# An eight-expert layer: every token through every expert in split precision, against tokens sorted by expert and moved by indirect transfers

## The reference

```python
logits_BSE = jnp.einsum('BSD,DE->BSE', x, router_kernel_DE)
probs_BSE = jax.nn.softmax(logits_BSE.astype(jnp.float32), axis=-1)
weights_BSK, indices_BSK = jax.lax.top_k(probs_BSE, TOP_K)          # TOP_K = 2 of E = 8
norm_weights_BSK = jax.nn.softmax(weights_BSK, axis=-1)
one_hot_BSKE = jax.nn.one_hot(indices_BSK, num_classes=E, dtype=x.dtype)
full_weights_BSE = jnp.sum(one_hot_BSKE * norm_weights_BSK[..., None], axis=2)
gating_BSEF = jnp.einsum('BSD,EDF->BSEF', x, kernel_gating_EDF)     # D = 256, F = 512
act_BSEF = jax.nn.silu(gating_BSEF)
up_BSEF = jnp.einsum('BSD,EDF->BSEF', x, kernel_up_EDF)
fuse_BSEF = act_BSEF * up_BSEF
down_BSED = jnp.einsum('BSEF,EFD->BSED', fuse_BSEF, kernel_down_EFD)
out_BSD = jnp.einsum('BSED,BSE->BSD', down_BSED, full_weights_BSE)
```

## Time and profile before

| | |
|---|---|
| median of 3 runs | 1378.36 us (1377.51 to 1386.43) |
| profiled execution, device time | 1375.61 us |
| its span in the trace | 1373.7 us |
| its mean granted TensorE clock | 0.891 of full speed |
| first work of the expert stage | 655.35 us |
| end of its last normalisation | 1033.46 us |

### The profile page before, as it was taken

One profiled execution on the slowest core, in us unless ns is written; L12 is line 12 of the kernel. 1 busy time (PEld: TensorE's weight loads), 2 busy tenths in 40 slices (PEclk: granted clock), 3 DMA queues, 4 the chain that ended last, 5 costly groups with the idle time before them and its releaser, 6 DMA issues. The chain is left out here.

```text
span 1373.7 us, 29227 instructions
## 1 busy us (share of the span) xinstructions
PE 1106.4 (81%) x11509; PEld 922.8 (67%) x11509; DVE 728.2 (53%) x1538; ACT 547.3 (40%) x1059; POOL 391.0 (28%) x466
## 2 busy tenths in 40 slices
PE   5899364899976565898889999999995899998373
PEld 5787233777753354786689999999994677777231
DVE  4467375566646997465254433434364445443374
ACT  2344271656527762453434232333221333332550
POOL 0222154444314442223211211211105444432102
PEclk9999586999988787999799999999998799996675
DMA  5100201000001000200110111030001000000001
GB/s 177 66 3 3 97 1 65 1 1 0 1 3 34 1 0 1 94 3 2 47 47 1 47 46 46 5 126 0 0 1 68 2 3 3 3 3 1 1 1 36
DMA packets 11140, 35.64 MB, mean 26 GB/s; under 512 B 3026, under 2 KB 5795, under 8 KB 9362
## 3 DMA queue, kind: packets, MB, share of 16 engines
q1 hardware_dynamic: 11026, 34.06, 7.0%
HBM read 32.84 MB, written 1.21 MB: 25 GB/s over the span
## 5 line engine op out<-in xcount | busy, mean ns | idle before, releaser
L147 PE MATMUL psum<-L2f_XT_high,L2f_EW_high 128*128 128x444 f32 (+1 forms) x384 | 136.8, 356 | 9.0 <-issue 5.1
L1929 ACT ACTIVATE L2f_act<-psum 128x444 f32<-128x444 f32 (+1 forms) x96 | 48.9, 511 | 222.6 <-PE psum L147 222.5
L147 PE MATMUL psum<-L2f_XT_high,L2f_EW_low 128*128 128x444 f32 (+1 forms) x384 | 134.8, 351 | 0.0
L147 PE MATMUL psum<-L2f_XT_low,L2f_EW_high 128*128 128x444 f32 (+1 forms) x384 | 134.3, 350 | 0.0
L2008 DVE TENSOR_TENSOR L2f_prod<-psum,L2f_act 128x444 f32<-128x444 f32 (+1 forms) x96 | 55.8, 582 | 148.1 <-ACT L2f_act L1929 148.1
L1894 POOL TENSOR_TENSOR L2f_EW_low<-weights_even,L2f_EW_high 128x1024 fp32r<-128x1024 f32 x24 | 58.1, 2424 | 265.5 <-ACT L2f_EW_high L1908 265.5
L147 PE MATMUL psum<-L2f_EW_high,L2f_H_high 128*111 128x256 f32 x352 | 99.3, 282 | 2.6 <-issue 2.6
L147 PE MATMUL psum<-L2f_EW_low,L2f_H_high 128*111 128x256 f32 x352 | 98.8, 281 | 0.0
L147 PE MATMUL psum<-L2f_EW_high,L2f_H_low 128*111 128x256 f32 x352 | 98.4, 280 | 0.0
L147 PEld LDWEIGHTS psum<-L2f_XT_high,L2f_EW_high 128*128 128x128 f32 x384 | 73.4, 191 | 15.5 <-issue 8.5
L147 PEld LDWEIGHTS psum<-L2f_XT_high,L2f_EW_low 128*128 128x128 f32 x384 | 73.3, 191 | 3.9
(11 more groups left out here) (359 smaller groups left out, 2797.0 us busy)
## 6 DMA issues: line engine op xcount, KB each, us to landing
weights_even<-experts SPq DMA_DIRECT2D x8, 1536.0 KB, 6.5
weights_even<-L_w SPq DMA_DIRECT2D x4, 1024.0 KB
patch_ring<-patches SPq DMA_DIRECT2D x11, 333.0 KB, 3.6
weights_odd<-L_wqkv SPq DMA_DIRECT2D x2, 768.0 KB
out<-X SPq DMA_DIRECT2D x10, 111.0 KB
weights_odd<-L_wo SPq DMA_DIRECT2D x1, 1024.0 KB, 9.9
weights_even<-tok_w SPq DMA_DIRECT2D x1, 768.0 KB
weights_even<-L_wg SPq DMA_DIRECT2D x1, 768.0 KB, 4.3
```

Of the source, the lines that this page charges most:

```text
L147: mm = core.nc.tensor.matmul(out, left[a], right[b], start=first and n == 0, stop=last and n == len(passes) - 1)
L1929: nc.scalar.activation(act_[:, p, 0:k * R], core.bank(p)[:, 0:k * R], ACT.Silu).then_inc(act_done, 1)
```

## The change

Each token's two (token, expert) pairs become two slots in a list sorted by expert, where each expert begins on a multiple of 128. The list has at most (2 x 1221 + 8 x 127) / 128 = 27 tiles of 128 slots (`NS`), and the program always runs 27. One expert serves a whole tile.

- SyncE copies `X` to DRAM twice, as `expert_rows` and as `expert_sums`, and loads all eight experts (12.6 MB) at the start of the stage. It then loads the next stage's weights, waits for the last addition, and reads `expert_sums` back into `X`.
- The ranks come from matmuls with matrices of ones, and the list from 22 matmuls that turn marks into the token (`source`, `target`) and weight (`wslot`) of each slot. VectorE makes the marks; it does some 35 instructions more than `route` did, and nothing runs beside them but the transfers.
- GpSimd gathers 128 rows for each tile into a ring of three buffers (`xs`) and adds 128 rows for each tile into `expert_sums`, by indirect transfers. An addition waits for the landing of the one before it.
- TensorE works in plain fp32 with one call for a product where it had three: per tile two transposes, two gate calls and two up calls of 512 columns, four transposes of the hidden tile, four down calls of 256 columns. The expert's number is read from SBUF into a register of TensorE (`value_load`) and picks the columns of `EW`.

Core of the diff, with the list's arithmetic left out:

```diff
+NS = (2 * TOK + 8 * 127) // 128
...
             @block.sync
             def _(sp):
-                with sp.Fori(0, (NEX - 2) // 2) as j:
-                    for u in range(2):
-                        sp.wait_ge(w_low, j * 6 + 3 * (u + 1))
-                        sp.dma_start(raw[u], core.dram["experts"][j * 2 + (2 + u)]).then_inc(we[u], 16)
+                for p in SPLIT:
+                    sp.dma_start(by_tile(rows, p, 0, NT), X[p, :, :]).then_inc(rows_out, 16)
+                for e in range(NEX):
+                    sp.dma_start(EW[:, e, :], core.dram["experts"][e]).then_inc(w_in, 16)
+                for p in SPLIT:
+                    sp.dma_start(by_tile(sums, p, 0, NT), X[p, :, :]).then_inc(sums_out, 16)
                 load_next(sp, next_loads, next_sem)
+                sp.wait_ge(added, 16 * NS)
+                for g, (t0, k) in enumerate(GROUPS):
+                    for p in SPLIT:
+                        sp.dma_start(X[p, t0:t0 + k, :], by_tile(sums, p, t0, k)).then_inc(back[g], 16)
...
             @block.gpsimd
             def _(pool):
...
+                def gather(j):
+                    if j == 0:
+                        pool.wait_ge(rows_out, 32)
+                        pool.wait_ge(source_done, 1)
+                    after(pool, x2_ps, j - 2)
+                    nc.gpsimd.indirect_dma_start(xs[:, j % 3, :], None, rows[:, :],
+                                                 bass.IndirectOffsetOnAxis(ap=source[:, j:j + 1], axis=0)).then_inc(got[j % 3], 16)
+
+                def scatter(j):
+                    if j == 0:
+                        pool.wait_ge(sums_out, 32)
+                        pool.wait_ge(target_done, 1)
+                    pool.wait_ge(y_done, j + 1)
+                    after(pool, added, 16 * j)
+                    nc.gpsimd.indirect_dma_start(sums[:, :], bass.IndirectOffsetOnAxis(ap=target[:, j:j + 1], axis=0), Y[:, j % 2, :], None,
+                                                 compute_op=ALU.add).then_inc(added, 16)
+
+                for j in range(3):
+                    gather(j)
+                for j in range(NS):
+                    scatter(j)
+                    if j + 3 < NS:
+                        gather(j + 3)
                 tail.pool(pool)
...
             @block.vector
             def _(dve):
...
+                def weigh(j):
+                    dve.wait_ge(y_ps, j + 1)
+                    after(dve, added, 16 * (j - 1))
+                    V.tensor_scalar(Y[:, j % 2, :], core.bank(5)[:, 0:D], wslot[:, j:j + 1], None, ALU.mult).then_inc(y_done, 1)
...
+                for g in range(len(GROUPS)):
+                    dve.wait_ge(back[g], 32)
+                    tail.stats(g)
+                for g in range(len(GROUPS)):
+                    tail.norm(dve, g)
...
             @block.tensor
             def _(pe):
...
+                def x_T(j):
+                    pe.wait_ge(got[j % 3], 16 * (j // 3 + 1))
+                    after(pe, x2_done, j - 1)
...
+                for j in range(NS + 1):
+                    if j + 1 < NS:
+                        x_T(j + 1)
+                    if j < NS:
+                        expert[j] = pe.value_load(expert_of[0:1, j:j + 1], min_val=0, max_val=NEX - 1)
+                        if j == 0:
+                            pe.wait_ge(w_in, 16 * NEX)
+                        pe.wait_ge(x2_done, j + 1)
+                        after(pe, silu_done, j - 1)
+                        half(j, j % 2, 0, g_ps)
+                    if j >= 1:
+                        pe.wait_ge(prod_done, j)
+                        after(pe, ht_done, j - 1)
+                        for c in range(4):
+                            mm = nc.tensor.transpose(core.bank(4)[:, c * 128:(c + 1) * 128], H[:, (j - 1) % 2, c * 128:(c + 1) * 128], core.ident[:, :])
+                        mm.then_inc(ht_ps, 1)
+                    if j < NS:
+                        after(pe, prod_done, j - 1)
+                        half(j, 2 + j % 2, KD * NF, u_ps)
+                    if j >= 1:
+                        pe.wait_ge(ht_done, j)
+                        after(pe, y_done, j - 1)
+                        for c in range(4):
+                            mm = nc.tensor.matmul(core.bank(5)[:, 0:D], HT[:, (j - 1) % 2, c * 128:(c + 1) * 128],
+                                                  EW[:, expert[j - 1], 2 * KD * NF + c * D:2 * KD * NF + (c + 1) * D], start=c == 0, stop=c == 3)
+                        mm.then_inc(y_ps, 1)
```

More of the change, by code:

```diff
@@ L1857, in experts_ffn @@
-        we = [we0, we1]
+        hot, spot = sb("hot", [128, 2, NT, NEX]), sb("spot", [128, 2, NT, NEX])
+        both, rank = sb("both", [128, NT, NEX]), sb("rank", [128, NT, NEX])
+        need = sb("need", [128, 8, NEX])
+        slot, which, inside = sb("slot", [128, 2, NT]), sb("which", [128, 2, NT]), sb("inside", [128, 2, NT])
+        ended, owner = sb("ended", [128, NS, NEX]), sb("owner", [128, NS])
+        expert_of = sb("expert_of", [128, NS], I32)
+        mark, empty, wslot = sb("mark", [128, NS]), sb("empty", [128, NS]), sb("wslot", [128, NS])
@@ L2100, in body @@
[L2100 to L2110 removed]
+                pe_transpose_x(core, pe, xt_ps, lambda t, c: X[:R, t, c * 128:(c + 1) * 128], core.ident[:R, :R], False, xt_done)
@@ new lines, in _ @@
+                for t in range(NT):
+                    pe.wait_ge(xt_done, t // 2 + 1)
+                    for c in range(KD):
+                        mm = nc.tensor.matmul(core.bank(0)[:R, t * NEX:(t + 1) * NEX], XT[:, c, t * R:(t + 1) * R], router[:, c, :],
+                                              start=c == 0, stop=c == KD - 1)
+                mm.then_inc(lg_ps, 1)
+                pe.wait_ge(both_done, 1)
+                pe.wait_ge(set_up, 1)
+                flat = both[:R].rearrange("p t e -> p (t e)")
@@ new lines, in _, with x_T, half @@
+                mm.then_inc(mark_ps, 1)
+                pe.wait_ge(owner_done, 1)
+                def x_T(j):
+                    pe.wait_ge(got[j % 3], 16 * (j // 3 + 1))
+                    after(pe, x2_done, j - 1)
+                    for c in range(KD):
+                        mm = nc.tensor.transpose(core.bank(6 + j % 2)[:, c * 128:(c + 1) * 128], xs[:, j % 3, c * 128:(c + 1) * 128], core.ident[:, :])
+                    mm.then_inc(x2_ps, 1)
+                def half(j, bank, first, sem):
+                    for c in range(KD):
+                        mm = nc.tensor.matmul(core.bank(bank), xsT[:, j % 2, c, :], EW[:, expert[j], first + c * NF:first + (c + 1) * NF],
+                                              start=c == 0, stop=c == KD - 1)
+                    mm.then_inc(sem, 1)
```

392 lines of the change are left out of this document (169 added, 223 removed).

## The result

| | before | after |
|---|---|---|
| median | 1377.93 us (4 runs, 1373.79 to 1386.43) | 1443.02 us (4 runs, 1437.58 to 1453.59) |
| ratio to before | | 1.0473, 95% interval 1.039 to 1.0556 |
| span of the profiled execution | 1373.7 us | 1435.2 us |
| mean granted TensorE clock | 0.891 | 0.812 |
| expert stage | 378.1 us | 435.5 us |

The change makes the kernel 4.7% slower. 1411 us was forecast, with a range of 1345 to 1505. Of any kernel here some executions run 1.5% or more above the fastest at a lower granted clock: the medians hold them, the ratios and their intervals leave them out.

A forecast was written before the change was run, and what follows sets the result against it. The prediction took TensorE's matmuls to bound the 378.1 us expert stage. The new stage, 43 + 162 + 176 + 8 + 4 + 18 = 411 us, adds 33 to 1375.6, 1408.6; with 2.8 for the median, 1411 us, range 1345 to 1505.

The forecast's parts named there:

- the sum: Expert stage: all terms together 411 us against 378.1, so +33, giving 1408.6 us for the profiled execution.
- What goes, and the products: Expert stage: all up and down passes, 365 us, go; new TensorE work is 6.0 us per tile, 162 us.
- The serial turn: Expert loop: TensorE idles 5.25 us in each of 24 turns, waiting for weighting, two issues and the gather's landing.
- The clock: Expert loop: idling lowers TensorE's clock and costs 2.1 us more per turn, from 1.5 to 2.7.
- The expert's number: Expert loop: reading it into TensorE's register costs 0.3 us for each of 27 tiles, 8 us.
- The start: Stage's start: transfers (42 us) and routing (43 us) must both end before the first expert matmul, 43 us.
- Speeding either alone would bring nothing: Stage's start: the transfer and routing paths, 42 and 43 us, are nearly equal, so shortening just one gains nothing.
- The end: After the last down product: last addition, reading X back, statistics and norms take 18 us.
- Short transfers: Rival, expert loop: GpSimd issues in 0.42 us, a turn idles 3.7 us, total 1358 us; chance 0.2.
- The ring hides the gathers: Rival, expert loop: three buffers hide the gathers, the 176 us go, total 1235 us; chance 0.04.
- Long transfers: Rival, expert loop: issues of 2.42 us and landing of 3.9, 9.5 us idle per turn, total 1529 us; chance 0.12.
- a clock that never rises: Rival, expert loop: TensorE's clock stays low, 6.0 us of work take 12, total 1505 us; chance 0.08.

The follow-up runs named there:

- e10: e3 with the expert of tile j fixed at j modulo 8 instead of read from SBUF: median 1241.94 us, 0.8992 of the time before the change.
- e2: The changed kernel with six dummy TensorE products in each of the 24 waits for a gather: median 1398.66 us, 1.0136 of the time before the change.
- e1: The changed kernel with each gather issued ahead of the addition in GpSimd's queue: median 1254.25 us, 0.9071 of the time before the change.
- e3: The changed kernel with four gather buffers instead of three, gathers still behind the additions: median 1247.82 us, 0.9018 of the time before the change.
- e6: e1 with dummy TensorE products between the router, rank and mark matmuls at the stage's start: median 1250.53 us, 0.9048 of the time before the change.
- e5: e1 with the next stage's weights held back until two additions have landed: median 1259.94 us, 0.9095 of the time before the change.
- e4: The changed kernel with a plain indirect write in place of the addition into DRAM: median 1431.47 us, 1.0382 of the time before the change.
- e9: e3 with one extra GpSimd power instruction and a drain after the last addition's issue: 1248.71 us, one run.
- e11: e9 with the edits of e5 and e6: median 1252.75 us, 0.9017 of the time before the change.

## Why the prediction was right

The forecast was slower, by 2.4%; measured is 4.7%. The mechanism is the one that it rests on, and of the 32 us between 1411 and 1443 the stage has 24.5 (435.5 against 411). The profiled execution took 1437.58 us, 29.0 above the 1408.6 of the sum, so 4.5 lie outside the stage (it begins 3.8 us later); the median is 5.4 above that execution, where I had put 2.8.

- **What goes, and the products.** Right. A full-speed turn was put at 6.0 us; e10's mean is 6.03 and most of its turns last 5.82, and its gate, up and down take 1.88, 1.88 and 1.89 with their modelled ends overlapping.
- **The serial turn.** Right: 24 waits of 5.25 us forecast, 24 of 5.85 measured. The terms: handoffs and weighting 0.78 forecast, 0.80 to the addition's issue; the addition's issue 1.2 against 1.59, the gather's 1.2 against 0.99, and a pause of 0.30 between two transfers that I had not; landing 2.05 against a mean of 2.14. No row had an issue's price: that 1.2, chosen between a SyncE issue and a big GpSimd instruction, came out within 0.2 us for the two together is luck, since the two errors nearly cancel.
- **The clock.** 2.1 us per turn forecast. From the first transpose to the last product pass 8.69 us in the change (881.19 to 889.88) and 6.72 in e2 (801.31 to 808.03): 1.97, of which 1.8 are the gate product's.
- **Where the turn was mis-sized.** With the expert's number a turn was put at 13.65 us; measured are 14.25, and the 0.6 more are idling, by the pause and the addition's issue above all. The other 8.4 us came out as forecast, though not by the forecast's terms. The work at full speed (5.8), the clock (1.97) and the number (0.16) are all a little less than I took. What fills up the rest I had not seen: after a late gather the transposes stand alone ahead of the gate product for 0.85 us, the number's 0.16 among them (881.19 to 882.04), where in e1 the one follows the other after 0.22. I had summed the work of a full pipeline and the wait of an empty one. The whole loop takes 362.6 us instead of 350.
- **The expert's number.** 8 us forecast, for which I gave a cover that isn't there: the load stands behind the transposes in TensorE's queue and not ahead of their wait. In the change it shows as 0.16 us per tile, 4.3 in all; in e10 against e3 as 8.7. The Trainium skill's page DMA: Bandwidth & Descriptors (Latency and other measured facts) has a floor of 600 ns for it, 16 us by that page's estimate; about half of that came out, or a quarter, and the loads' own records last 0.30 us.
- **The start.** 43 us forecast, 51.4 measured, 8.4 of the 24.5 us by which the stage was off. Sized by records that carry columns, 44 router records of 8 columns had 3 us and took 8.25, and ranks and marks had 9 and took 14.7: in the start's window the weight loads are busy for 26.87 us and the products for 27.97, so records so short last as long as their weight loads, at half clock. The first gather had 4.4 us with its transposes; from the list at 700.74 to the first expert product at 710.54 it took 9.8, with the transfer engines 81% busy (701 to 711). VectorE's steps had 15.2 us and took 9.2.
- **"Speeding either alone would bring nothing."** Wrong as put. TensorE did not wait for the experts' weights, the last of which land at 698.6, 39.4 us into the stage; e6, which speeds the routing alone, wins 5.3 us at the start and keeps them. Wrong too is that the next stage's weights cost nothing: the first gather runs against them, and e5, which holds them back, has its first product 3.8 us earlier.
- **The end.** 18 us forecast, 21.5 measured (1073.14 to 1094.68). The 2.98 us that the last addition waits for the one before and GpSimd's pause, of which 1.82 us hold VectorE up, were not in the sum.
- **The rivals.** Short transfers: the issues are neither 0.42 us nor 2.42, and the change would have had to lose less than 6.0 us per turn to win; it loses some 8. The rule of the Trainium skill's page DMA: Bandwidth & Descriptors (Anatomy of one DMA, the GpSimd path) puts a whole transfer of this size at 2.3 us, an estimate by that page. From a gather's issue to its use pass 2.9, and the addition takes 1.59 before that. As a latency of one transfer it is not far off; what it leaves out is that GpSimd is occupied for the issue. The ring hides the gathers: it would have needed one more buffer (e3) or the other order (e1), and 1235 us, the price put on it, is near the 1248 of e3. Long transfers and a clock that never rises: neither occurred.

## What to carry to other kernels

A prefetch counts in the distance from issue to use along the queue that issues it: if the issue stands behind a wait for the end of the current turn, three buffers prefetch nothing, and one swapped line is worth 13% of the kernel. When an engine is half idle, read its clock too, because here a quarter of what each turn lost was work done at a lower clock, and dummy products in the idle stretches gave that part back. A transfer moved out of one crowded stretch has to be looked for in the next.

## What the runs showed of the hardware

- An indirect transfer of 128 rows of 1 KB occupies GpSimd for 0.99 us as gather or plain write and 1.59 us with an addition, with 0.30 us between two of them; in the change a gather lands 1.7 to 2.9 us after its issue has ended, and the first three, with the transfer engines 81% busy, after 5.0 to 5.1. The slower ones (2.2 us and more) belong to the same nine tiles in the change, in e2 and in e4, which points at the list of rows or the tile's place in it; neither was tried.
- After a row of indirect transfers GpSimd stands still for 4.6 us behind its first elementwise instruction, ahead of the first power, in the nine versions with such transfers that issue no power early, and not in the two that do (e9, e11). Whether the transfers bring it on, and whether it must be a power, was not tried.
- Reading a number from SBUF into TensorE's register (a record of 0.30 us) and picking columns by it costs about 0.3 us between two products.
- 44 fp32 records of 8 columns take 8.25 us at half clock, 0.19 us each.
